# Layer-1 attention, global rounds: score units, value groups and side pieces in another order on TensorE

## What is computed

```python
def sdpa(q, k, v, mask):                       # 16 heads of 8, 4 key/value heads
    scores = einsum('bhqd,bhkd->bhqk', q, k) / sqrt(8)
    probs = softmax(where(mask, scores, -1e30))
    return einsum('bhqk,bhkd->bhqd', probs, v)
x = x + global_latent_attn(rmsnorm(x, norm1_w), ...)   # causal mask, all 1024 positions
x = x + local_gqa_attn(rmsnorm(x, norm2_w), ...)       # causal, window of 32
```

## Time and profile before

| | us |
|---|---|
| median of 3 runs | 2619.33 |
| lowest and highest | 2613.45, 2625.76 |
| the profiled execution | 2615.01 |
| its span, first to last instruction | 2613.3 |
| global rounds of layer 1 within it | 1666.9 to 2050.1 |
| TensorE busy | 2304.5 (88%) |
| VectorE busy | 1548.6 (59%) |
| ScalarE busy | 1233.7 (47%) |
| GpSimd busy | 953.9 (37%) |

### The profile page before, as it was taken

How to read it: one execution, slowest core, us unless ns; L and a number is a source line. 1 busy time by engine, 2 the same in 40 slices (tenths; PEclk the granted TensorE clock), 3 DMA queues, 4 the chain that set the end, 5 groups by cost and what they waited for, 6 DMA issues and landing times. The chain is left out here.

```text
span 2613.3 us, 41691 instructions
## 1 busy us (share of the span) xinstructions
PE 2304.5 (88%) x15308; PEld 1392.4 (53%) x15308; DVE 1548.6 (59%) x3383; ACT 1233.7 (47%) x1733; POOL 953.9 (37%) x925
## 2 busy tenths in 40 slices
PE   5999999999999999756999995699999989937586
PEld 2555565556555655445888883334344444524464
DVE  4676757766777577543666667445555445356534
ACT  2555536553655454312333331577877655613241
POOL 0777757775777577610000002223223211000001
PEclk9999999999999999965999997699999988968798
DMA  2000000000000000020000000000000000020001
GB/s 70 1 1 1 1 1 1 1 1 1 1 1 1 1 1 1 1 61 1 0 0 0 0 1 6 1 1 1 1 1 1 1 1 1 2 75 0 0 1 32
DMA packets 35462, 18.03 MB, mean 7 GB/s; under 512 B 15323, under 2 KB 33125, under 8 KB 35301
## 3 DMA queue, kind: packets, MB, share of 16 engines
q1 hardware_dynamic: 35300, 15.86, 2.4%
HBM read 13.76 MB, written 2.10 MB: 6 GB/s over the span
## 5 line engine op out<-in xcount | busy, mean ns | idle before, releaser
L311 POOL TENSOR_TENSOR a_first<-a_first,a_ring 128x512 f32<-128x512 f32 (+3 forms) x352 | 559.9, 1591 | 141.9 <-ACT a_ring L556 106.6
L1576 ACT ACTIVATE g_probsT<-g_s_ps 128x1024 f32<-128x1024 f32 (+2 forms) x448 | 381.8, 868 | 150.3 <-PE g_s_ps L1460 86.6
L556 ACT ACTIVATE a_ring<-a_st 128x768 f32<-128x768 f32 (+1 forms) x256 | 234.8, 917 | 262.8 <-PE a_st L463 262.8
L478 PE MATMUL a_o_ps<-a_ring,a_v 128*64 128x512 f32 (+3 forms) x1280 | 249.2, 485 | 3.2 <-POOL a_ring L293 2.2
L1485 PE MATMUL g_o_ps<-g_probsT,g_values 128*32 128x512 f32 (+5 forms) x2688 | 231.8, 423 | 20.9 <-ACT g_probsT L1576 16.8
L645 DVE RECIPROCAL a_row_inv<-a_row_inv 128x512 f32<-128x512 f32 x64 | 213.7, 3341 | 16.8 <-ACT a_row_inv L544 16.8
L1045 ACT ACTIVATE m_silu<-m_up,m_bias 128x512 f32<-128x512 f32 x160 | 110.1, 688 | 238.8 <-PE m_up L1012 238.8
L1012 PE MATMUL m_up<-m_xT_hi,m_w_hl 128*128 x640 | 211.9, 402 | 7.1 <-DVE m_glu L1061 4.3
L623 DVE TENSOR_REDUCE a_part_max<-a_mx 128x2 f32<-128x1024 f32 x128 | 156.5, 1223 | 103.1 <-PE a_mx L434 99.6
L1460 PE MATMUL g_s_ps<-g_qT,g_kT 64*128 64x512 f32 (+3 forms) x896 | 208.0, 463 | 10.3 <-ACT g_probsT L1576 9.1
L1343 POOL TENSOR_SCALAR_AFFINE_SELECT g_probsT<-g_probsT 128x512 f32<-128x512 f32 x128 | 88.2, 689 | 271.9 <-ACT g_probsT L1576 271.5
(11 more groups left out here) (285 smaller groups left out, 4156.4 us busy)
## 6 DMA issues: line engine op xcount, KB each, us to landing
m_w<-in_L_ffn_rw SPq DMA_DIRECT2D x2, 1024.0 KB, 8.3
s_w<-in_L_ffn_w SPq DMA_DIRECT2D x1, 2048.0 KB, 10.6
s_w<-in_L_ffn_w SPq DMA_DIRECT2D x4, 512.0 KB, 10.4
out_x<-x SPq DMA_DIRECT2D x4, 512.0 KB, 3.2
m_w<-in_L_ffn_rw SPq DMA_DIRECT2D x2, 512.0 KB, 7.6
x<-in_L_attn_x SPq DMA_DIRECT2D x1, 512.0 KB, 4.2
a_outT<-in_L_attn_w_q SPq DMA_DIRECT2D x1, 512.0 KB, 5.0
a_outT<-in_L_attn_w_k SPq DMA_DIRECT2D x1, 512.0 KB, 5.7
```

The costliest lines, as they stand in the source:

```text
L311: pool.tensor_tensor(total[:, h, q:q + w], total[:, h, q:q + w], probs_of(n, u)[:, h, off:off + w], ALU.add).then_inc(added, 1)
L478: last = pe.matmul(o_ps[rows_of(h), first_q:first_q + w], v_half[n // 4 % 2][:, j, head:head + A_HD], probs_of(n, u)[:, h, off:off + w], s ...
L556: act.activation(probs_of(n, u)[:, :, 0:w], st_ps[u % 2][:, :, 0:w], ACT.Exp).then_inc(exp_done, 1)
L1576: act.activation(out, src.rearrange("p k (j n) -> p k j n", j=at_once), ACT.Exp, scale=float(HD) ** -0.5).then_inc(exp_done, 1)
```

## The change

Only `global_pair` is changed. The instructions and their numbers stay the same, as do the waits in front of each; their order in TensorE's queue is another. Two score units stand in a row, then both late value groups, then two score units, then both side pieces, then the fifth score unit and the pair's own value group. Local steps are as before.

```diff
-                    late_r, late_n = (r, n - 2) if n else (r - 1, STEPS - 2)
-                    for i, (m, unit) in enumerate(units):
-                        score(r, m, unit)
-                        if i == 0 and late_r >= 0:
-                            weigh(late_r, late_n, 1)
-                        if i == 1 and late_r >= 0:
-                            weigh(late_r, late_n + 1, 0)
-                        if i == 2:
-                            fill_banks(r, n)
-                        if i == 3:
-                            fill_banks(r, n + 1)
+                    for i in (0, 1):
+                        score(r, *units[i])
+                    if r or n:
+                        weigh_last_of(*((r, n - 2) if n else (r - 1, STEPS - 2)))
+                    for i in (2, 3):
+                        score(r, *units[i])
+                    fill_banks(r, n)
+                    fill_banks(r, n + 1)
+                    score(r, *units[4])
                     weigh(r, n, 0)
```

## The result

The changed kernel takes 2607.8 us (median of 6 runs, 2605.1 to 2612.0); the kernel before, with three runs more, 2620.0. The ratio is 0.9955, with a 95% interval of 0.9934 to 0.9977: 12 us less, where 17 were forecast. A second set of 7 runs gave 0.9961 [0.9946, 0.9975]. The median lies in the range; the gain, just under the 13 us that was set as the bound of what can be told, is told apart from zero by both intervals.

A forecast was written before the change was run, and what follows sets the result against it. TensorE sets the pace in layer 1's global rounds; about 41 us of saved exits, cut by exponential waits to 20, less 3 us of deductions, gives 17 us less: 2619.3 to 2602 us, range 2591 to 2610.

The forecast's parts named there:

- the price of a change of kind: TensorE, global rounds: switching between score, value-group and side-piece matmuls costs 0.21 us leaving a score, 0.15 leaving the others.
- 0.72 us of exits a pair: Each pair of steps goes from ten blocks to six, saving two exits from scores, one value-group and one side-piece exit.
- B: Pair type with key blocks 1 and 6; forecast to go from 5.35 to 4.76 us, gain 0.58.
- D to A: Border from pair (3,4) to pair (0,7): the second score waits for the last exponential, 0.8 us waited away.
- A: Pair type with key blocks 0 and 7; forecast 6.2 to 6.3 us against 6.17, gain about 0.15 on average.
- C: Pair type with key blocks 2 and 5; forecast to go from 5.33 to 4.89 us, gain 0.46.
- layout: Global rounds laid out block by block from trace durations, with waits for exponentials: 20 us gained over four rounds before deductions.
- How much the exponentials take: Global rounds: waits for exponentials cut the saved exits from about 41 us to 20.
- What was taken off: Deductions of 1 us each: tile changes in projections, the causal-cut wait at step 6, and moved side pieces.
- rival (c): The clock falls at D to A borders, 1.5 us a fall: net slower, 2626 or 2650 us; chance 0.09.
- Rival (a): Waits for exponentials and causal cuts cover nearly all the gain: 3 to 8 us less, 2613; chance 0.16.
- Rival (b): Hardly any new wait in the global rounds: 30 to 40 us less, 2584; chance 0.05.

The follow-up runs named there:

- A apart: Against the changed kernel, the old front (S W S W) for A pairs alone, the rest as changed; 2600.7 us, ratio 0.9917 to the kernel before.

## Why the prediction was right, and where it was off

- **What bounds these rounds and the price of a change of kind**: right. 0.21 after a score, 0.15 after a value group or side piece gave the blocks to 0.02 us. Only the reading behind the 0.21, that the first of two scores streams for 0.22, is off: the second starts 0.34 after it. What two scores in a row save, 0.20, is as forecast, and the sum goes by that.
- **No work is added; 0.72 us of exits a pair**: right where nothing waits. B went from 5.35 to 4.72, 0.63 of the 0.72; with halved exponentials 0.69 came back.
- **The exponential is late next, at D to A**: right in place. At step 24 A took 6.11 (6.2 to 6.3 was forecast), with its second score 0.82 after the first (0.9); B 4.72 (4.76), C 4.93 (4.89). But at step 8 A took 5.51 and hardly waited, and C at steps 4 and 20 took 5.36 and 5.53, where waits for scores, a cut and a side bank came together. A middle round without a fall took 91.18, where the layout with its deductions had 95.9 - 4.7 = 91.2; that it fits to 0.1 is in part luck, since A gained 0.6 more and C 1.3 less than laid out, and the deductions took up the difference. The last round took 85.98.
- **How much the exponentials take**: too high. The forecast lost 21 of the 41 us to them, and its layout gave back 15 on halving them; measured were 7 (rounds) to 12 us (runs), and the waits for cuts and side banks, which the forecast put at 2 to 3, are what holds next.
- **What was taken off**: the wait at step 6 grew from 0.91 to 1.42 and not to 2; VectorE's side banks added 1.3 us and the new queries 0.6. The sum of 3 was about right.
- **The sum, 17 us**: 19 by the rounds, 16 at equal low time, 12 as measured. What lies between is rival (c), the clock, which the forecast had as an alternative of 9 in 100 and counted at nothing within its own sum. That is the term that was mis-sized: it was not all or nothing. Low time was 369 us on average (standard error 3) against 361 (1), worth 3 us. By the prediction's own signs it came: a granted clock under 0.97 in a middle round, 0.95 in the first profile, though 1.00 and 0.98 in the second. Its price for a fall, 1.5 us, held, and its place, D to A, is borne out at step 24. But that the new order brought all the 8 us is not shown: in the profiles only 14 to 28 us of low time lie in its rounds (18 in the kernel before), and outside them, where nothing was changed, it was 332 us before and 346 and 337 after.
- **Rival (a)**, waits that cover nearly all: no. **Rival (b)**, no new wait: no.
- **One sign was misjudged**: "TensorE's waits for ScalarE up by some 20 us". The list shows 3, for the two reasons given above. I would look at starts. The "middle rounds of about 90.5 us" left out the deductions that the forecast had made.
- The forecast gave 0.65 to a gain of more than 13 us and 0.29 to one within 13 us of nothing. The gain of 12 falls just into the second, less likely part.

What stays open: why a kernel's mean low time differs from another's, since most of it lies outside the global rounds and a profile is one execution; and why A apart is 3.5 us faster than the changed kernel at equal low time when its rounds are 1 us shorter at most.

## What to carry to other kernels

Group matmuls of one tile shape, but only as far as the engine that feeds the next one allows: with two buffers and an exponential of 0.92 us, two scores side by side are free only where some 1.8 us of other work follows, and where the work was short, at D to A, little of the gain was left at three of four borders. Read the price of a change of kind from start to start and lay the new order out block by block with the consumer's durations, but lay out the other engines' queues too: an order found on paper that left GpSimd and VectorE out gained half or less of what it promised over the change (6.3 us for 13). Compare orders by rounds in which the clock did not fall; medians of whole runs mixed in 3 to 10 us of clock. A short wait on TensorE can be followed by a fall of the clock that costs more (1.4 us) than the wait (0.5 to 0.9); filling the wait with matmuls that nobody reads was followed by a better clock here, though it made each middle round 1 us longer.

## What was not expected of the hardware

- With 48 matmuls more, 0.23 us apart, the kernel was 6 us faster in the median (2601.0 against 2607.4, of different sets of runs and another chip; 0.9924 against 0.9961 in ratio), at a mean granted clock of 0.932 and not 0.930.
- A cut of GpSimd that takes 0.64 us elsewhere took 1.27 at 1818.20 us in the kernel before, while VectorE did two products of the rotation (1817.40 to 1818.97, 0.82 and 0.83 us):

```profile
1818.20 1.27 POOL L1343 TENSOR_SCALAR_AFFINE_SELECT g_probsT<-g_probsT 128x512 f32<-128x512 f32 x1 [7.13 <-ACT g_probsT L1576]
```

It is so in all four rounds (1.25 to 1.27 us, each beside these two products), while each of the 60 cuts that VectorE's work hardly overlaps takes 0.64. That VectorE's work slows it is likely from this; no run separates the two.
